# Head values in wide products, and norms folded into the stages before them, in a two-block decoder on one core

## What is computed

```
h = x + mamba(norm(x));  h = h + cross0(norm(h), ctx);  h = h + experts0(norm(h))
h = h + attn1(norm(h));  h = h + cross1(norm(h), ctx);  h = h + experts1(norm(h))
cross1: q, k, v; per head norm of q and k; 16 heads of softmax(q k^T / sqrt(32)) v; output projection and bias
```

## Time and profile before

| | us |
|---|---|
| three runs | 3736.28, 3744.59, 3748.47 |
| median | 3744.59 |
| profiled execution, its own time | 3736.67 |
| its span | 3734.9 |
| PE busy, share of the span | 3272.4, 88% |
| DVE | 2426.2, 65% |
| ACT | 1765.0, 47% |
| POOL | 1206.5, 32% |

### The profile page before, as it was taken

The page is one execution under the profiler, slowest core; times in us unless marked ns, Lnnn a source line. Parts: engine busy times, 40 slices in busy tenths (PEclk is TensorE's granted clock), DMA queues, the critical chain, the costliest instruction groups (busy, mean ns, idle before and its releaser), DMA issues. The chain is left out here.

```text
span 3734.9 us, 37930 instructions
## 1 busy us (share of the span) xinstructions
PE 3272.4 (88%) x12581; PEld 1665.4 (45%) x12581; DVE 2426.2 (65%) x4463; ACT 1765.0 (47%) x3318; POOL 1206.5 (32%) x962
## 2 busy tenths in 40 slices
PE   3740799999999799999999999799899889999964
PEld 3320344444444454554545554344444446555532
DVE  8769899999998555555555555533322358777654
ACT  4748566666664343343433433343201137767521
POOL 0433799999996010100000000123582020000014
PEclk9975899999999899999999999899999999999977
DMA  7125335253522212222111110446430120000046
GB/s 252 58 62 163 139 99 149 90 147 99 143 91 97 74 60 74 74 69 81 49 62 51 59 57 29 147 136 214 138 104 29 40 79 1 1 1 1 1 151 215
DMA packets 201331, 334.88 MB, mean 90 GB/s; under 512 B 25648, under 2 KB 76208, under 8 KB 198064
## 3 DMA queue, kind: packets, MB, share of 16 engines
q1 hardware_dynamic: 187904, 298.69, 24.8%
q0 software_dynamic: 12208, 33.57, 3.2%
q10 hardware_dynamic: 1024, 0.20, 0.0%
HBM read 217.69 MB, written 114.69 MB: 89 GB/s over the span
## 5 line engine op out<-in xcount | busy, mean ns | idle before, releaser
L1235 POOL TENSOR_TENSOR sc_dBu<-sc_dtu,xa 128x1024 f32<-128x1024 f32 x256 | 540.0, 2131 | 38.6 <-DMA sc_dtu<-scan_dtu 29.4
L1145 PE MATMUL y_ps<-sc_g,ident 128*128 128x512 f32 x1024 | 476.3, 600 | 18.6 <-POOL sc_g L1223 12.1
L1259 DVE TENSOR_TENSOR_SCAN sc_dA<-sc_dA,sc_dBu 128x1024 f32<-128x1024 f32 x160 | 365.1, 2282 | 6.9 <-POOL sc_dBu L1235 6.9
L1485 ACT ACTIVATE c_p<-c_ps,c_sm 128x512 f32<-128x512 f32 x256 | 195.6, 774 | 354.1 <-DVE c_sm L1526 354.1
L1525 DVE TENSOR_REDUCE c_sm<-c_ps 128x4 f32<-128x2048 f32 x64 | 146.7, 2292 | 312.4 <-PE c_ps L1448 312.4
L1199 ACT ACTIVATE sc_dA<-sc_dt,a_neg 128x511 f32<-128x511 f32 x512 | 329.6, 676 | 11.2 <-DVE sc_g L1259 9.8
L1145 PEld LDWEIGHTS y_ps<-sc_g,ident 128*128 128x128 f32 x1024 | 189.8, 190 | 256.6 <-issue 168.1
L1518 DVE SCALAR_TENSOR_TENSOR xa<-c_ps,c_sm,xa 128x512 f32<-128x512 f32 x256 | 192.1, 751 | 147.4 <-PE c_ps L1439 133.7
L1439 PE MATMUL c_ps<-c_wo,c_oT 128*128 128x512 f32 x512 | 246.5, 605 | 2.3 <-DVE xa L1518 1.6
L1420 PE MATMUL c_ps<-c_xT,c_wq 128*128 128x512 f32 x512 | 232.9, 598 | 5.1 <-DMA c_wq<-in_c_wq_dram 5.1
L1467 PE MATMUL c_ps<-c_pT,c_v 128*128 128x512 f32 x512 | 230.9, 594 | 2.4 <-DVE c_pT L1537 2.4
(11 more groups left out here) (497 smaller groups left out, 6250.6 us busy)
## 6 DMA issues: line engine op xcount, KB each, us to landing
kv_w<-in_c_wkv_dram SPq DMA_DIRECT2D x32, 512.0 KB, 4.3
cross_keys<-kv_out SPq DMA_DIRECT2D x64, 256.0 KB, 2.0
cross_values<-kv_out SPq DMA_DIRECT2D x128, 128.0 KB, 1.9
c_kT<-cross_keys SPq DMA_DIRECT2D x64, 256.0 KB
c_rk<-cross_rk SPq DMA_DIRECT2D x64, 256.0 KB
c_v<-cross_values SPq DMA_DIRECT2D x64, 256.0 KB
expert_rows<-e_yt SPq DMA_DIRECT2D x63, 256.0 KB, 2.0
xa<-scan_bc SPq DMA_DIRECT2D x48, 256.0 KB, 8.1
```

The source lines that it names most:

```text
L1145: ins = pe.matmul(yps[:, k % 2, :], ident[:], g[:, c % GS, n, :], start=False, stop=(m == NCH - 1 and n == NG - 1))
L1235: pool.tensor_tensor(dBu[:, c % 3], spread(dtu[:, k % DT, :], NG), bc[:, m * NG:(m + 1) * NG, :], ALU.mult).then_inc(s_dBu, 1)
L1259: dve.tensor_tensor_scan(to.rearrange("p n s -> p (n s)"), dA[:, c % 2].rearrange("p n s -> p (n s)"), dBu[:, c % 3].rearrange("p n s -> p ...
L1485: ins = act.activation(pr[:, j, :], ps[:, SB + j, :], ACT.Exp, scale=rq[:, j:j + 1], bias=bias[:, j:j + 1], accum_out=l[:, j:j + 1])
```

## The change

- Out_proj and the norm c0 are one stage. A class `Norm` gives each engine its part for one tile. Statistics follow each drain, scales follow tiles 8, 14 and 16; products use four banks and not eight. `g2` is loaded behind the four loads of x, and DVE waits for it ahead of its first drain; `wT` is loaded in cross0 behind the weights of its head 1.
- Experts0: `EARLY` is (2, 7, 8), so that two more products go ahead. The norm a1 is in its tail: statistics behind each tile's sum, transposes between products from `TURN` = 24 on, eight tiles behind the last. The loads of the attention are issued at its own start, ahead of its keys and values.
- Qkv1: `keyed(b + 1)` is ahead of `normalise(b)`.
- Heads1: transposed probabilities are kept for a set, in five places for queries, and the values of four heads and 512 queries are 16 products of 512 columns, once a set, behind the transposes of the next set's second step. Outputs are in four steps in a row, 5 to 8 of the next batch. The ring of probabilities has three places, not four. A result is copied by ACT in one or two parts.

The core of the diff:

```diff
+class Norm:
...
+    def measured(self, dve, own, t):
+        own.after(dve.bn_stats(self.st[:, t, :], self.xa[:, t, :]))
+        own.after(dve.bn_aggr(self.mv[:, t, :], self.st[:, t, :]))
+
+    def scales(self, dve, own, g):
+        lo, hi = self.groups[g], self.groups[g + 1]
+        v, t, r = self.rs[:, 0, lo:hi], self.rs[:, 1, lo:hi], self.rs[:, 2, lo:hi]
+        own.after(dve.tensor_scalar(v, self.mv[:, lo:hi, 1], 1e-5, None, ALU.add))
+        rsqrt(dve, own, r, v, t)
+        dve.scalar_tensor_tensor(out=v, in0=self.mv[:, lo:hi, 0], scalar=-1.0, in1=r, op0=ALU.mult,
+                                 op1=ALU.mult).then_inc(self.s_rs, 1)
+
+    def applied(self, act, t):
+        act.wait_ge(self.s_rs, sum(lo <= t for lo in self.groups))
+        if t >= self.ring:
+            act.wait_ge(self.s_tr, t - self.ring + 1)
+        act.activation(self.xn[:, t % self.ring, :], self.xa[:, t, :], ACT.Identity, scale=self.rs[:, 2, t:t + 1],
+                       bias=self.rs[:, 0, t:t + 1]).then_inc(self.s_xn, 1)
+
+    def turned(self, pe, t):
+        n = len(self.banks)
+        if t >= n:
+            pe.wait_ge(self.s_cp, t - n + 1)
+        pe.wait_ge(self.s_xn, t + 1)
+        for c in range(HC):
+            ins = pe.transpose(self.banks[t % n][:, c * P:(c + 1) * P], self.xn[:, t % self.ring, c * P:(c + 1) * P],
+                               self.ident[:])
+        ins.then_inc(self.s_tr, 1)
+
+    def copied(self, act, t):
+        act.wait_ge(self.s_tr, t + 1)
+        act.activation(self.xT[:, :, t * P:(t + 1) * P],
+                       self.banks[t % len(self.banks)].rearrange("p (c t) -> p c t", c=HC), ACT.Copy).then_inc(self.s_cp, 1)
...
+                sp.dma_start(g2[:], A["gqk"]).then_inc(s_g2, 16)
...
-                    if t >= 8:
-                        pe.wait_ge(s_out, t - 7)
+                    if t >= 4:
+                        pe.wait_ge(s_out, t - 3)
...
+                    if t >= 10:
+                        norm.turned(pe, t - 10)
+                for t in range(NB * TT - 10, NB * TT):
+                    norm.turned(pe, t)
+
+            @block.scalar
+            def _(act):
+                for t in range(NB * TT + 2):
+                    if t < NB * TT:
+                        norm.applied(act, t)
+                    if t >= 2:
+                        norm.copied(act, t - 2)
 
             @block.vector
             def _(dve):
...
+                kept()
+                dve.wait_ge(s_g2, 16)
+                dve.tensor_tensor(gqk[:], g2[:, 0:1], g2[:, 1:2], ALU.mult)
...
+                    dve.wait_ge(s_out, t + 1)
+                    norm.measured(dve, own, t)
+                    if t + 1 in GROUPS:
+                        norm.scales(dve, own, GROUPS.index(t + 1) - 1)
...
-        norm_all(nc, "c0", xa, xT, ident, loads=[
-            (g2[:], A["gqk"]), (wT[:], A["e0_wT"].rearrange("(c p) n -> p c n", p=P))])
...
-EARLY = (2, 6, 6)
...
-                    if n == EARLY[2]:
+                    if n == EARLY[2] + 2:
                         pe.wait_ge(s_ye, TL)
                     product(n)
+                    if n >= TURN:
+                        norm.turned(pe, n - TURN)
+                for t in range(HALVES - TURN, NTT):
+                    norm.turned(pe, t)
 
...
+                act.wait_ge(s_de, TL)
                 for n in range(EARLY[2], HALVES):
                     taken(n)
+                    if n >= TURN - 2:
+                        norm.applied(act, n - TURN + 2)
+                    if n >= TURN:
+                        norm.copied(act, n - TURN)
+                for t in range(HALVES - TURN, NTT):
+                    if t + 2 < NTT:
+                        norm.applied(act, t + 2)
+                    norm.copied(act, t)
 
...
+                    if k:
+                        dve.wait_ge(s_out, n + 1)
+                        norm.measured(dve, own, j)
+                        if j + 1 in GROUPS:
+                            norm.scales(dve, own, GROUPS.index(j + 1) - 1)
...
-        norm_all(nc, "a1", xa, xT, ident, keep=xn, loads=loads)
...
+                for i, (to, src) in enumerate(loads):
+                    sp.dma_start(to, src).then_inc(s_w if i < HC else s_b, 16)
...
+            keyed(0)
             for b in range(NB):
                 taken(b)
+                if b + 1 < NB:
+                    keyed(b + 1)
                 normalise(b)
-                keyed(b)
...
-    RING = 4
+    RING, PLACES = 3, TT + 1
...
-    pT = ctx.enter_context(nc.sbuf_tensor("h1_pT", [P, 2, 2, TT, P], F32))
-    oT = ctx.enter_context(nc.sbuf_tensor("h1_oT", [P, 2, HC, S], F32))
+    pT = ctx.enter_context(nc.sbuf_tensor("h1_pT", [P, HG, TT, PLACES, P], F32))
+    oT = ctx.enter_context(nc.sbuf_tensor("h1_oT", [P, HC, S], F32))
...
-    def finished(s):
-        b, r = divmod(s, BATCH)
-        return (b - 1, r // SET) if b and r % SET == SET // 2 else None
+    def slot(k, j):
+        return TT if j == 0 and k % 2 else j
+    def filled(e):
+        return e // SET - 1 if e >= SET and e % SET == 1 else None
+    def finished(e):
+        b, r = divmod(e, BATCH)
+        return (b - 1, r - 5) if b and 5 <= r < 5 + TT else None
...
-            def values(s):
-                b, g, j, heads = place(s)
-                pe.wait_ge(s_ea, s + 1)
-                if s and s % SET == 0:
-                    pe.wait_ge(s_Oe, s // SET)
+            def values(k):
+                b, g = divmod(k, HC)
+                pe.wait_ge(s_ea, (k + 1) * SET)
+                if k:
+                    pe.wait_ge(s_Oe, k)
                 for kt in range(TT):
-                    for i, h in enumerate(heads):
+                    for h in range(HG):
                         n = g * HG + h
-                        ins = pe.matmul(ps[h * HD:(h + 1) * HD, OB, j * P:(j + 1) * P],
-                                        v[:, b, kt, n * HD:(n + 1) * HD], pT[:, s % 2, i, kt, :], start=(kt == 0),
-                                        stop=(kt == TT - 1))
+                        ins = pe.matmul(ps[h * HD:(h + 1) * HD, OB, :], v[:, b, kt, n * HD:(n + 1) * HD],
+                                        pT[:, h, kt, k % 2:k % 2 + TT, :].rearrange("p j q -> p (j q)"),
+                                        start=(kt == 0), stop=(kt == TT - 1))
                 ins.then_inc(s_O, 1)
             def output(b, j, bank):
...
-                    ins = pe.matmul(ps[:, bank, :], oT[:, b % 2, g, j * P:(j + 1) * P], wo[:, g, :], start=(g == 0),
+                    ins = pe.matmul(ps[:, bank, :], oT[:, g, j * P:(j + 1) * P], wo[:, g, :], start=(g == 0),
...
-            for s in range(N + 3):
+            for s in range(N + 2):
                 if s + 1 < N:
                     scores(s + 1)
-                if 2 <= s < N + 2:
-                    transposes(s - 2)
-                if s >= 3:
-                    values(s - 3)
-                    if finished(s - 3):
-                        output(*finished(s - 3), YB)
+                if s >= 2:
+                    e = s - 2
+                    transposes(e)
+                    if filled(e) is not None:
+                        values(filled(e))
+                    if finished(e):
+                        output(*finished(e), YB)
+            values(N // SET - 1)
             for j in range(TT):
                 output(NB - 1, j, YB - j % 2 * 4)
         @block.scalar
         def _(act):
-            def gathered(s):
-                b, r = divmod(s, BATCH)
-                act.wait_ge(s_O, s + 1)
-                act.activation(oT[:, b % 2, r // SET, :], ps[:, OB, :], ACT.Copy).then_inc(s_Oe, 1)
-            for s in range(N + 3):
+            def gathered(k):
+                b, g = divmod(k, HC)
+                act.wait_ge(s_O, k + 1)
+                if g == 0 and b:
+                    act.wait_ge(s_Y, b * TT)
+                if k % 2:
+                    act.activation(oT[:, g, P:S], ps[:, OB, 0:S - P], ACT.Copy)
+                    act.activation(oT[:, g, 0:P], ps[:, OB, S - P:S], ACT.Copy).then_inc(s_Oe, 1)
+                else:
+                    act.activation(oT[:, g, :], ps[:, OB, :], ACT.Copy).then_inc(s_Oe, 1)
+            for s in range(N + 2):
...
-                if 2 <= s < N + 2:
+                if s >= 2:
                     e = s - 2
+                    k, r = divmod(e, SET)
+                    j, pair = divmod(r, PAIRS)
                     act.wait_ge(s_T, e + 1)
-                    if e >= 2:
-                        act.wait_ge(s_O, e - 1)
-                    act.activation(pT[:, e % 2].rearrange("p i k q -> p i (k q)"), ps[:, PT:PT + 2, :],
-                                   ACT.Copy).then_inc(s_ea, 1)
-                if s >= 3 and (s - 3) % SET == SET - 1:
-                    gathered(s - 3)
+                    if k and r == PAIRS:
+                        act.wait_ge(s_O, k)
+                    act.activation(pT[:, 2 * pair:2 * pair + 2, :, slot(k, j), :],
```

(39 more changed lines are left out.)

136 lines of the change are left out of this document (79 added, 57 removed).

## The result

The changed kernel took 3703.47 us (3696.62 to 3703.98) against 3746.53 for the kernel before on the same chip: ratio 0.9884, interval 0.9864 to 0.9904. It is faster by 43 us; the forecast was 3686, range 3664 to 3716. The profiled run has a span of 3702.1, 32.8 less than the one of before.

The account below looks back on a forecast made before the run. PE was taken as the bound, busy 3272.4 of 3734.9 us, read stage by stage. Terms −21.1 − 6.6 − 22.9 − 5.6 = −56.2 from 3736.67 gave 3680.5, plus 5.5 for a low profiled run: 3686, range 3664 to 3716.

Parts of the forecast that it names:

- the burst: Heads: 16 products of 512 columns once in eight steps, four strips beside each other, taking 3.6 us, 1.66 of it added.
- the first batch: Heads: the first batch, 24×2.80 + 3×4.46, was to take 2.6 us less, its first set having no burst.
- The clock is no such case: Heads: a lowered clock was ruled out as a slower case, since PE busy 7.64 of 12 us was granted 0.99.
- D: The heads: values leave each step, a burst once in eight steps is added; −21.1 us, range −24 to −8.
- The prediction's own signs: Wrong if burst over 4.9, heads' granted clock under 0.9, or DVE's statistics outlast experts0's products; heads 452 us, weight at 1247.
- two tiles through ACT, PE and copy: Out_proj's end: behind DVE's scales at 1243.0 only two tiles were left for ACT, PE and copy, to 1246.3.
- 3 if they land late: Attention's start: ten weight and bias loads that lose their cover cost nothing, or 3 us if they land late.
- Rival 4: A, B and C bring half, as g2, stores and attention's loads end late: −39, 3703; part of the forecast's 0.76.
- A: Out_proj with its norm: −6.6 us, range −12 to 0.
- B: Experts0 into attention, two more products early and the norm in the tail: −22.9 us, range −26 to −15.
- C: Order in qkv1, keyed(3) ahead of normalise(3): −5.6 us, range −6 to −2.
- the forecast's own case: Heads: four strips of columns run beside each other in the burst; total 3686, chance 0.76.

Follow-up runs that it names:

- d_undone: The changed kernel with the heads stage of the kernel before: 3716.55 us, ratio 0.9931 to the kernel before.
- fed: The changed kernel with four unread plain products at the heads' start and one more in each of steps 1 to 8: 3691.98 us, ratio 0.9865.
- early_undone: The changed kernel with the two more early products of experts0 back in its tail, the norm still fused: 3713.56 us, ratio 0.9926.
- two_wide: The changed kernel with the 16 products reordered, heads 0 and 1 first, then heads 2 and 3: 3733.56 us, ratio 0.9981.
- d_alone: The kernel before with only the heads stage of the changed kernel: 3737.91 us, ratio 0.9973.

## Why the forecast was right, and where it was off

- **Heads, the burst: right.** 3.57 for a forecast of 3.6; DVE's step with it 4.43 for 4.46; a batch with outputs 107.4 for 108.3. The four score products of four heads at once were the row that carried it. By the rate of 0.88 a product the burst runs at an estimated 16×0.88/3.57 = 3.9 times one strip. The Trainium skill, "TensorE: Matmul & The Clock Gate", Part 3: Packing small matmuls, has 3.07 for four row tiles; no run here shows that little for four strips of columns.
- **Heads, the first batch: the step that failed.** Forecast 2.6 less, measured 7.3 more, in a sum of 21.1 forecast and 12.4 measured. (The forecast's terms for this batch, 24 steps of 2.80 and three of 4.46, are 27 of its 32 steps; only with the other five does −2.6 come out.) The forecast let the clock go with "The clock is no such case", on a row that shows a full clock *held* by a lightly loaded TensorE. It is held here too: 1.00 in 3111 to 3150 with 32.92 of 39 busy. What it didn't ask is how the clock comes back once it has fallen, as it does at this stage's start in both kernels, where TensorE waits 2.6 to 3.2 us ahead of its first and its second scores. In the kernel before it came back 2.6 us behind the first values (3092.47), some 16 us in (in d_undone 7 us behind them, 21 in); the changed loop has only scores and transposes until its ninth step's burst (3105.33), and is granted 0.50 through 38 us in which PE is busy for every one (32.00 of 32.00, 6.00 of 6.00). It comes back 2.6 us into that burst. The run fed has 1.00 from 3063 and gets 9.9 us back. The Trainium skill, same page, Part 4: PE-mode transpose, says that transposes don't count as work for the clock as other matmuls do; the rows agree with it, but no run here has transposes alone.
- **Heads, the rest of the 8.7 us that D fell short.** The end cost 1.6: the last batch gave 2.4 (forecast 1.6), but the tail took 1.7 more and not 0.7 less, with the last burst at 0.50 too (5.33 us) behind waits of 1.1 to 1.7. The two middle batches gave 10.7 and 8.9 where 8.1 each were forecast, since the first of them took 118.15 before and not 116.4. DVE's first step came 0.7 later.
- **The prediction's own signs.** It said it would be wrong with a granted clock under 0.9 in the heads. Over the whole stage it is 0.93, over the first 48 us 0.50. The heads, from the first to the last instruction, take 461 us and not 452, the first weight of cross0 is issued 56.7 after out_proj's start (1256.23) and not 52.5, and the attention starts 17.7 earlier against the stage before it and not 23.
- **Out_proj: the wait right, its tail wrong.** DVE's first drain came 13.6 after the stage's start, forecast 14.0, PE waited 5.91 for it, and the last scales ended 49.7 after the start, forecast 48.2. But then the forecast had "two tiles through ACT, PE and copy". ACT had eight: the second scales come for six tiles at once at 1243.3, ACT needs 1.18 each for these and the last two, and ends at 1255.2, 55.6 after the start instead of 51.5. Of these 4.1, DVE's chain has 1.5 and ACT's tail 2.6. That is read from the rows; no run changed the groups of the scales. With 61.2 as the mean of three runs of before and 59.2 of nine with this stage, the step gave −2.0 and not −6.6, inside its range.
- **Experts0: right in the mean, 5 short in its own profile.** Against the profile that the forecast started from it gave −17.7, with 8.8 us of waits for stores where 4 were taken. Between the means of three and of eight it is −24.3, and the attention behind it takes 1.4 more in the mean (323.4 to 326.2, where it took 323.4 before). The loads that lost their cover are the likely reason (forecast "3 if they land late"), but no run moved them. That is −22.9 in all, the forecast to the tenth, by chance. The waits are 6 to 9 with the changed stage and its ring of three, and 3 to 13 before. The clock that the early products kept up (early_undone) was in no term.
- **Qkv1:** −4.3 between means (92.3, 88.0), −5.4 by the run that undid it: as forecast, within 1.3.
- **Total.** The parts by means are −2.0 − 24.3 + 1.4 − 4.3 − 12.4 = −41.6, the runs say −43, the forecast's sum −56.2. It missed by 8.7 in the heads, 4.6 in out_proj and 1.3 in qkv1; the other 4 of the 17 us between 3686 and 3703.5 lie in the kernel before, taken as 3742 and measured here as 3746.5. Rival 4 names 3703, the time that came, and that is luck: A, B and C brought 29 of 35 and not half, and it was D that fell short. Chances: the forecast's own case (four strips at once) came true, and 13 us were lost to things that no rival named, above all a clock that doesn't come back.

## What to carry to other kernels

When an edit takes work from the engine with a throttled clock, ask two things of the clock: will the lighter load hold it, and can the lighter load bring it back where it has fallen. Here they had different answers, and only the rows in which it *rises* tell the second. When one group of scales frees several tiles at once, count the tiles that the next engine has still to do, not those of the last group. And before a stage's gain is priced in one profile, look for waits in it that differ from run to run: here one stage of unchanged code took 272 to 285 us.

## What the runs showed of the hardware

- With scores and transposes only, TensorE stayed at the lower of its two levels (0.50, 1.2 GHz) for 38 us in which it never paused, and the same loop stayed at the full level (1.00, 2.4 GHz) once it had it: 3111 to 3129 with 14.62 of 18 busy. With plain products in the loop it stood at 1.00 from 3063; with four at the start alone it was back at 0.50 behind a stretch of 2 us in which PE was busy for 0.63.
- The level fell in the middle of experts0 too: behind waits of 3.22 and 4.76 us it was 0.50 in 2389 to 2402 (early_undone), and behind the changed kernel's wait of 7.17 us it was 0.50 in 2588 to 2592.
- Four strips of 32 columns with 512 columns of float32 each run at an estimated 3.9 times one. By the starts of the records in two_wide, strips start their own streams without waiting for others that stand ahead of them in the program (the second train at 3221.75, the first still starting records at 3222.16 and later).
- Stores of 256 KB issued beside gathers made ScalarE idle 8.55 us in the changed kernel and 13.49 in d_alone, and PE by a sum that differs from profile to profile of the same code: 3.3, 7.4 and 12.9 in three, over all fourteen 3.3 to 12.9.
